# A sample's products in five matmuls instead of six: 126 rows in two planes of s, with 14 rows moved by DMA

## The reference, cut to what matters

```
a   = relu(group_norm(conv1x1(x, w1)))                       # 256 channels
om  = conv3x3(a, w_off) + b_off                               # 27 channels: 9 dx, 9 dy, 9 masks
for each tap k of 9 and pixel p:
    sampled[:, k, p] = mask[k, p] * bilinear(a, p + tap k + (dy, dx)[k, p])   # 0 outside
out = relu(group_norm(einsum(sampled, w2)))
out = relu(group_norm(conv1x1(out, w3)) + x)
```

## Time and profile before

| | us |
|---|---|
| median of 3 runs | 2962.01 (2961.58 to 2963.43) |
| the profiled execution | 2961.04 |
| its span, first to last instruction | 2958.8 |

### The profile page before, as it was taken

The page is one execution under the profiler, slowest core; times in us unless marked ns, Lnnn a source line. Parts: engine busy times, 40 slices in busy tenths (PEclk is TensorE's granted clock), DMA queues, the critical chain, the costliest instruction groups (busy, mean ns, idle before and its releaser), DMA issues.

```text
span 2958.8 us, 46593 instructions
## 1 busy us (share of the span) xinstructions
PE 2908.3 (98%) x16518; PEld 2865.9 (97%) x16518; DVE 2366.0 (80%) x5000; ACT 1795.0 (61%) x3281; POOL 455.3 (15%) x305
## 2 busy tenths in 40 slices
PE   9999999999998999999999999999999999999997
PEld 9999999999997899999999999999999999999997
DVE  5655889865666688888888888888888888888885
ACT  4544332346665466767666676676766767667664
POOL 0000000000000122221222212222122221222210
PEclk9999999999999899999999999999999999999998
DMA  7774111035663344444444444444544444444431
GB/s 270 215 238 134 44 44 40 10 124 218 245 232 130 122 136 152 156 150 158 150 153 154 148 159 151 153 155 150 158 150 156 152 149 159 148 152 156 149 121 74
DMA packets 209208, 437.39 MB, mean 148 GB/s; under 512 B 18640, under 2 KB 170192, under 8 KB 203344
## 3 DMA queue, kind: packets, MB, share of 16 engines
q1 hardware_dynamic: 159408, 326.82, 32.7%
q10 hardware_dynamic: 49568, 107.60, 11.8%
HBM read 307.71 MB, written 126.64 MB: 147 GB/s over the span
## 4 chain that ended last, share of the span: by engine, by line
PE 63%; DVE 3%; DMA 1%; ACT 1%; SPq 0%; issue 0%; POOL 0%; ACTq 0%; DVEq 0%; POOLq 0%
PE sample L87 7%; PE deform L87 7%; PE sample L88 7%; PE sample L92 7%; PE deform L92 7%; PE deform L88 6%; PE work L87 6%; PE work L92 6%; PE work L88 6%; PE work L74 1%; PE work L76 1%; PE work L75 1%; DMA hats<-hat_scratch 1%; PE work L2046 1%; DVE x L1715 1%; DVE s_lo L1819 1%
## 5 line engine op out<-in xcount | busy, mean ns | idle before, releaser
L1465 ACT ACTIVATE v_hi<-sample 128x392 fp32r<-128x392 f32 (+1 forms) x640 | 291.7, 463 | 315.1 <-PE sample L92 306.0
L87 PE MATMUL sample<-s_hi,aT_hi 98*128 98x392 f32 (+1 forms) x1280 | 417.5, 331 | 8.9 <-DVE v_lo L1827 8.9
L1675 POOL TENSOR_TENSOR hats<-hats 98x784 f32<-98x784 f32 x160 | 341.0, 2131 | 523.1 <-DMA hats<-hat_scratch 504.3
L88 PE MATMUL sample<-s_hi,aT_lo 98*128 98x392 f32 (+1 forms) x1280 | 413.3, 328 | 0.0
L87 PE MATMUL deform<-v_hi,w_w 128*128 128x392 f32 x1152 | 403.5, 350 | 0.0
L88 PE MATMUL deform<-v_hi,w_w 128*128 128x392 f32 x1152 | 393.1, 341 | 0.0
L1827 DVE TENSOR_TENSOR v_lo<-sample,v_hi 128x392 fp32r<-128x392 f32 (+1 forms) x640 | 326.9, 518 | 66.5 <-ACT v_hi L1465 62.2
L92 PE MATMUL sample<-s_lo,aT_hi 98*128 98x392 f32 (+1 forms) x1280 | 315.1, 327 | 0.0
L92 PE MATMUL deform<-v_lo,w_w 128*128 128x392 f32 x1152 | 310.4, 342 | 0.0
L1456 ACT ACTIVATE s_hi<-hats 98x784 fp32r<-98x784 f32 x288 | 245.4, 852 | 98.5 <-DVE x L1715 71.7
L1819 DVE TENSOR_TENSOR s_lo<-hats,s_hi 98x784 fp32r<-98x784 f32 x288 | 281.1, 976 | 2.4 <-ACT s_hi L1456 1.4
(11 more groups left out here) (227 smaller groups left out, 7282.9 us busy)
## 6 DMA issues: line engine op xcount, KB each, us to landing
hats<-hat_scratch SPq DMA_DIRECT2D x768, 150.1 KB
x<-in_x SPq DMA_DIRECT2D x64, 784.0 KB, 5.8
in_home<-y_scratch ACTq DMA_DIRECT2D x248, 196.0 KB, 3.3
out<-x ACTq DMA_DIRECT2D x62, 784.0 KB, 4.4
y_home<-in_x SPq DMA_DIRECT2D x32, 784.0 KB, 5.0
y_scratch<-y_out SPq DMA_DIRECT2D x16, 1568.0 KB, 5.9
terms<-in_x SPq DMA_DIRECT2D x30, 784.0 KB, 4.7
y_scratch<-y_home SPq DMA_DIRECT2D x15, 1568.0 KB, 5.1
```

The costliest lines, as they stand in the source:

```text
L87: nc.tensor.matmul(out, w_hi, x_hi, start=start, stop=False)
L88: nc.tensor.matmul(out, w_lo, x_hi, start=False, stop=False)
L1465: nc.scalar.activation(v_hi[:, group % 2, c, 0:taps_of(g), i, :], sample[:, t % 2, 0:cols(g)].rearrange("p (k s) -> p k s", s=PIX), ACT.Co ...
L1675: nc.gpsimd.tensor_tensor(hats[:, slot, 0:2, 0:n], hats[:, slot, 0:2, 0:n], hats[:, slot, 2:3, 0:n].broadcast_to([HALF, 2, n]), ALU.mult). ...
```

## The change

The 196 pixels are cut 126 + 70 (`UPPER` 9 rows of y, `LOWER` 5) instead of 98 + 98. `hats`, `s_hi` and `s_lo` keep two planes, now of 126 rows: plane 0 the upper 126 pixels, plane 1 the lower 70 and, in rows 70 to 125, the first 56 of those again. `aT` has four planes: a_hi upper, a_lo upper, [a_hi lower; a_lo lower's first 56], [a_hi lower; a_lo lower's last 14]. A tile is then five matmuls of 126, 126, 126, 126 and 84 rows, 588 in all. What stands in the same rows of another plane has to change its partition, and a DMA does that: `copy_s` moves 14 rows of s_hi (392 elements each) into s_lo's plane 1 once per unit, `copy_aT` moves a_lo's rest in two DMAs per image, out of `aT_rest`, which lies in the space of a_f. A unit's hats take four DMAs instead of three, unit 8's eight instead of six. `part_aT` and `rest_aT` are two instructions each. The fifth matmul of a unit's first tile waits for the copy of s. Two semaphores for it, and one for aT, are taken over from the first layer (`used_before`; the hunks that hand them over are left out here).

```diff
-ROWS = SIDE // 2
+UPPER = 9
+LOWER = SIDE - UPPER
+A_ROWS = UPPER * SIDE
+R_ROWS = LOWER * SIDE
+TWICE = A_ROWS - R_ROWS
+C_ROWS = R_ROWS + R_ROWS - TWICE
...
-        aT_hi = sb("aT_hi", [HALF, 2, 2, CMID], F32R)
-        aT_lo = sb("aT_lo", [HALF, 2, 2, CMID], F32R)
+        aT = sb("aT", [A_ROWS, 2, 4, CMID], F32R)
...
-        hats = sb("hats", [HALF, HATS, 3, 2 * PIX])
-        s_hi = sb("s_hi", [HALF, 2, 2, 2 * PIX], F32R)
-        s_lo = sb("s_lo", [HALF, 2, 2, 2 * PIX], F32R)
...
+        hats = sb("hats", [A_ROWS, HATS, 3, 2 * PIX])
+        s_hi = sb("s_hi", [A_ROWS, 2, 2, 2 * PIX], F32R)
+        s_lo = sb("s_lo", [A_ROWS, 2, 2, 2 * PIX], F32R)
...
+        aT_rest = a_f[0:R_ROWS, :, :, 0:P].bitcast(F32R)
...
-            return 48 * (lap + 1 + (p.n + u // (UNITS - 1) if slot == HATS - 1 else 0))
+            return 64 * (lap + 1 + (p.n + u // (UNITS - 1) if slot == HATS - 1 else 0))
...
+                parts = [(i, slice(0, n))]
...
+                    parts = [(i, slice(i * PIX, (i + 1) * PIX)) for i in range(2)]
+                for i, at in parts:
+                    n = at.stop - at.start
+                    y_hat, x_hat = (hats_at[p.n % 2, e, i, :, t0:t0 + n] for e in range(2))
+                    for dst, rows in ((hats[:, slot, 0, at], slice(0, UPPER)), (hats[0:R_ROWS, slot, 1, at], slice(UPPER, SIDE)),
+                                      (hats[R_ROWS:A_ROWS, slot, 1, at], slice(UPPER, SIDE - 1))):
+                        sp.dma_start(dst, y_hat[rows].unsqueeze(1).broadcast_to([rows.stop - rows.start, SIDE, n])
                                      ).then_inc(hats_loaded[slot], 16)
-                    return
-                for half in range(2):
-                    src = hats_at[p.n % 2, 0, i, half * ROWS:(half + 1) * ROWS, t0:t0 + n]
-                    sp.dma_start(hats[:, slot, half, 0:n], src.unsqueeze(1).broadcast_to([ROWS, SIDE, n])
+                    sp.dma_start(hats[:, slot, 2, at], x_hat.unsqueeze(0).broadcast_to([UPPER, SIDE, n])
                                  ).then_inc(hats_loaded[slot], 16)
-                src = hats_at[p.n % 2, 1, i, :, t0:t0 + n]
-                sp.dma_start(hats[:, slot, 2, 0:n], src.unsqueeze(0).broadcast_to([ROWS, SIDE, n])
-                             ).then_inc(hats_loaded[slot], 16)
+            @of_pair
+            def copy_s(p, u):
+                unit = UNITS * p.n + u
+                sp.wait_ge(s_lo_made, unit + 1)
+                sp.dma_start(s_lo[R_ROWS:C_ROWS, unit % 2, 1].bitcast(F32), s_hi[TWICE:R_ROWS, unit % 2, 1].bitcast(F32)
+                             ).then_inc(s_moved[unit % 2], 16)
+            @of_pair
+            def copy_aT(p, i):
+                sp.wait_ge(aT_lo_made, 2 * p.n + i + 1)
+                if i == 1:
+                    sp.wait_ge(aT_moved, aT_moved_before + 64 * p.n + 32)
+                for plane, rows in ((2, slice(0, TWICE)), (3, slice(TWICE, R_ROWS))):
+                    n = rows.stop - rows.start
+                    sp.dma_start(aT[R_ROWS:R_ROWS + n, i, plane].rearrange("p (k c) -> p k c", k=KM).bitcast(F32),
+                                 aT_rest[rows, :, i].bitcast(F32)
+                                 ).then_inc(aT_moved, 16)
 
...
+                copy_s(now, 1)
                 load_hats(now, 4)
+                copy_s(now, 2)
                 load_hats(now, 5)
+                copy_s(now, 3)
                 load_hats(now, 6)
+                copy_s(now, 4)
                 load_hats(now, 7)
                 load_x(coming, 0)
+                copy_s(now, 5)
                 load_hats(now, 8)
                 load_x(coming, 1)
+                copy_s(now, 6)
+                copy_s(now, 7)
                 store_hats(after, 1, 0)
...
                 load_hats(after, 0)
                 load_hats(after, 1)
+                copy_s(now, 8)
                 load_hats(after, 2)
+                copy_aT(after, 0)
+                copy_s(after, 0)
                 load_hats(after, 3)
+                copy_aT(after, 1)
...
-                nc.scalar.activation(aT_hi[:, i].rearrange("p h c -> p (h c)"), work[0:HALF, 2 * i, :],
+                nc.scalar.activation(aT[:, i, 0], work[0:A_ROWS, 2 * i, 0:CMID], ACT.Copy)
+                nc.scalar.activation(aT[0:R_ROWS, i, 2:4],
+                                     work[0:R_ROWS, 2 * i, CMID:2 * CMID].unsqueeze(1).broadcast_to([R_ROWS, 2, CMID]),
                                      ACT.Copy).then_inc(aT_hi_made, 1)
...
-                nc.vector.tensor_tensor(aT_lo[:, i].rearrange("p h c -> p (h c)"), work[0:HALF, 2 * i, :],
-                                        aT_hi[:, i].rearrange("p h c -> p (h c)").bitcast(F32),
+                nc.vector.tensor_tensor(aT[:, i, 1], work[0:A_ROWS, 2 * i, 0:CMID], aT[:, i, 0].bitcast(F32),
+                                        ALU.subtract)
+                rest = work[0:R_ROWS, 2 * i, CMID:2 * CMID].rearrange("p (k c) -> p k c", k=KM)
+                nc.vector.tensor_tensor(aT_rest[:, :, i], rest,
+                                        aT[0:R_ROWS, i, 2].rearrange("p (k c) -> p k c", k=KM).bitcast(F32),
                                         ALU.subtract).then_inc(aT_lo_made, 1)
...
-                for h in range(2):
-                    products_of_high(nc, sample[:, t % 2, 0:n], aT_hi[:, i, h, c * P:(c + 1) * P],
-                                     aT_lo[:, i, h, c * P:(c + 1) * P], s_hi[:, unit % 2, h, at:at + n], start=(h == 0))
+                to, a_part = sample[:, t % 2, 0:n], aT[:, i, :, c * P:(c + 1) * P]
+                high, low = s_hi[:, unit % 2, :, at:at + n], s_lo[:, unit % 2, :, at:at + n]
+                nc.tensor.matmul(to, a_part[:, 0], high[:, 0], start=True, stop=False)
+                nc.tensor.matmul(to, a_part[:, 1], high[:, 0], start=False, stop=False)
+                if t in (0, 2):
+                    pe.wait_ge(aT_moved, aT_moved_before + 64 * p.n + 32 * (i + 1))
+                nc.tensor.matmul(to, a_part[:, 2], high[:, 1], start=False, stop=False)
                 if c == 0:
                     pe.wait_ge(s_lo_made, unit + 1)
-                for h in range(2):
-                    last = product_of_low(nc, sample[:, t % 2, 0:n], aT_hi[:, i, h, c * P:(c + 1) * P],
-                                          s_lo[:, unit % 2, h, at:at + n], stop=(h == 1))
+                nc.tensor.matmul(to, a_part[:, 0], low[:, 0], start=False, stop=False)
+                if c == 0:
+                    pe.wait_ge(s_moved[unit % 2], s_moved_before[unit % 2] + 16 * (unit // 2 + 1))
+                last = nc.tensor.matmul(to, a_part[0:C_ROWS, 3], low[0:C_ROWS, 1], start=False, stop=True)
                 last.then_inc(sampled, 1)
```

33 lines of the change are left out of this document (15 added, 18 removed).

## The result

| | before | after |
|---|---|---|
| median of the runs, us | 2961.8 (4 runs) | 3466.3 (4 runs, 3463.0 to 3469.0) |
| ratio, 95% interval | | 1.170, 1.168 to 1.172 |
| profiled execution, us (span) | 2961.0 (2958.8) | 3465.6 (3463.4) |
| mean granted clock over the span | 0.994 | 0.930 |

The kernel is 505 us slower, 17%, where 233 us (8%) had been forecast; the sign was right, the time lies 186 us above the top of the range. One execution among all that are reported here, of experiment e8b, ran in a slower state (3838 us at a mean granted clock of 0.67) and is left out of its median.

What follows compares the result with a forecast made beforehand. The prediction took a 61.6 us ring, with TensorE not alone on the path, as the bound. Parts of 48.1, 6.05 and 15.0 made 69.1 us, 7.5 more, times 31 = 233, giving 3195 us; 8-in-10 range 3000 to 3280.

Steps and rivals of the forecast that it cites:

- three parts of a ring: The 61.6 us step: tile 5 to tile 16's end 43.45, then to unit 0's s_lo 5.55, then to tile 5 12.6.
- Unit 4's load: Behind image 1's aT DMAs on SP: costs nothing, as VectorE takes unit 4 after unit 2's s_lo; bound 1 us.
- aT, +0.5 us a step: Split copy on ScalarE (+0.35) and split subtraction on VectorE (+0.15) lengthen tile 16's end to unit 0's s_lo to 6.05.
- Four loads, +1.2 us of transfer, +0.77 of issue, in effect +1.2 at unit 3: A unit's fourth hats load shares DMA engines with the others, adding 1.2 us a unit; bounds 0 and 1.5.
- Unit 2's copy, 1.9 us: Between unit 2's s_lo and tile 4's fifth matmul: the copy lands 1.9 us on, so tile 5 starts after 15.0, not 12.6.
- Units 1, 3, 4, 5 and 7, nothing: Their copies cost nothing: more time in hand before the fifth matmul than unit 6 and less ahead in the queue.
- The issue of a copy, 0.45: On SP: issuing a copy of s takes 0.45 us, the x load's figure, and delays unit 3's load by that.
- Unit 6, stall 2.9 behind the x load: At tile 12's fifth matmul: the copy queues behind the second x load's 784 KB, landing 1619.6; stall 2.9 us.
- Unit 8, stall 3.8 behind loads 0 and 1: At tile 16's fifth matmul: the copy lands behind the next pair's unit 0 and 1 loads, at 1636.6; stall 3.8 us.
- The clock: Rival, 0.10: a 3.8 us stall could drop TensorE to half clock once a step, losing 2.7 us more; 3279 us.
- Copies don't queue: Rival, 0.20: each copy lands 1.9 us after issue, tiles 12 and 16 stall 0.5 each; step 63.4, total 3017 us.
- Faster: Rival, 0.10: hats loads come no later than now and nothing in flight delays a copy; step 61.0, total 2943 us.

Runs made afterwards that it cites:

- e8b: e1 with the two DMAs of aT's rest for image 0 issued ahead of unit 2's loads instead of behind them: 3096.5 us.
- e1: The changed kernel without the copies of 14 rows of s and without TensorE's wait for them: 3031.9 us.
- e2: The kernel before the change with the last of its six matmuls per tile left out, nothing else touched: 2915.9 us.
- e13: e1 with the third of a unit's four hats loads (56 rows) issued for the first three units only: 2960.4 us.
- e14: e1 with the third of a unit's four hats loads cut to an eighth of its columns: 3005.8 us.
- e10: e1 with the nine copies back in SP's list, into rows no product reads; TensorE waits for none, only ScalarE's part_s for the copy two units before: 3158.4 us.
- e9: e1 with the DMAs of aT's rest, and the waits for them, for the first pair only: 3044.3 us.
- e4: The changed kernel with ScalarE's two output stores issued later, behind write_y 0 and write_y 4: 3418.9 us.
- e7b: The changed kernel with unit 6's copy moved ahead of the second x load and unit 8's ahead of the next pair's unit 1 loads: 3252.1 us.
- e12: e11 with unit 2's copy also moved up, ahead of unit 4's loads: 3434.4 us.
- e15: e11 with ScalarE's second output store also moved, behind write_y 4: 3171.8 us.
- e6b: The changed kernel with the second product of tiles 4, 12 and 16 repeated (20, 16, 16 times) where TensorE would wait: 3364.6 us.
- e11: e7b with ScalarE's first output store issued later, behind write_y 0: 3164.9 us.

## Why the prediction was right about the sign and wrong about the size

The prediction added the step up from three parts of a ring. Measured in the traces by the same marks, as means of the steps between 1300 and 2800 us, they are:

| us a step | before | forecast | after | e1, no copies |
|---|---|---|---|---|
| end of s_lo of unit 0 to tile 5 | 12.9 | 15.0 | 19.0 | 15.6 |
| of it, to the end of s_lo of unit 2 | 11.0 | 12.84 | 12.9 | 12.7 |
| tile 5 to the end of tile 16 | 43.4 | 48.1 | 54.8 | 43.4 |
| the rest | 5.4 | 6.05 | 5.0 | 4.7 |
| step | 61.7 | 69.1 | 78.7 | 63.6 |

Of the 9.6 us a step that were missed, 4.0 lie between s_lo of unit 2 and tile 5, and 6.7 between tile 5 and tile 16; the rest of the ring came out 1.1 shorter than forecast. In the second part the stalls make 8.0 us where 6.7 were priced, matmuls at the lower clock 4.4 and the edges of stalls 1.2, where nothing was. From s_lo of unit 2 to tile 5 it is 6.1 us after (the flight of unit 2's copy is 5.7 of them), 1.9 before, and 2.9 in e1, which has no copies: there something else has grown. It is VectorE's wait for loads of hats, here before and after from 1300 to 2800 us (total, times, longest), which the point *Unit 4's load* below reads:

```profile
DVE hats L1812 <- DMA hats<-hat_scratch: 2.2, 5, 0.7
```
```profile
DVE hats L1856 <- DMA hats<-hat_scratch: 96.3, 45, 6.1
```

The runs split the 505 us another way: -46 (five matmuls, e2), +44 (aT's operations and 126 rows, e13 less e2), +45 and +26 (issue and bytes of the fourth load, e14 less e13, e1 less e14), +127 (copies issued, nobody waiting, e10 less e1), +308 (the fifth product waits for them). These are differences along one order of the edits; in another order the shares would differ, as 336 against 434 for the copies shows. Point by point:

- *Where TensorE would wait*: right for tiles 4, 12 and 16, and right that this turns a gain into a loss. Wrong in order: longest at tile 4, then 12, then 16. The 1.3 us at tile 0 did not come.
- *Five matmuls*: 2.1 us of the 3.3 lie in the ring's first part, 65 us. Measured 46.
- *aT, +0.5 us a step* in the last part of the ring: that part did not grow. 44 us are 1.4 a step, with the 126 rows, which I had priced at nothing, and they lie where unit 4's load is waited for (see *Unit 4's load*). *aT's two DMAs, nothing*: right as a cost (e9), though TensorE does wait for them; the place for this wait was not seen.
- *Four loads, +1.2 us of transfer, +0.77 of issue, in effect +1.2 at unit 3*: the place was right, since s_lo of unit 2 ended 12.9 us after that of unit 0, as forecast. Over the whole step 71 us are 2.3, and the larger part (45 of 71) is the issue and the fixed part, not the bytes on shared engines on which I had built.
- *Unit 2's copy, 1.9 us*: this step failed. Free of traffic a copy takes 2.1 us, so the bare price was good; but in its place it took 5.7. I wrote that a copy "moves behind what the same queue has in flight" and did not apply it here: unit 4's four loads stand between the copies of units 1 and 2 in the new list, and e4, with the store away, still has 4.4 us. And I never asked what ScalarE's queue sends at that moment. Its store of the output, 784 KB, stood in the earlier trace rows, used only as a bound for another transfer; e7b, with the loads out of the way, still has 4.2.
- *Unit 4's load, nothing*: this failed too. It was to be covered, as VectorE takes unit 4 up only behind s_lo of unit 2. Behind aT's DMAs and the copies of units 0 and 1 its first load is issued 8.1 us after the end of s_lo of unit 0, where it was 4.9 before, and VectorE then stands idle ahead of make_s of unit 4 in every step, 3.6 us on the mean (0.05 before; 1.3 in e1 and still 1.3 in e13 with its three loads). In the kernel after, the copy's flight hides this wait; without the copies it decides when tile 5 starts. That is why e1 is slower than e2, and why unit 2's copy could not simply be moved ahead of these loads (e12). Of the sign that the prediction gave, VectorE waiting over 1.5 us for unit 3, only 0.4 came; it waited for unit 4.
- *Units 1, 3, 4, 5 and 7, nothing*: failed for unit 3 (4.0 us behind the second store, 1.2 of stall) and, by little, unit 5 (0.4, its copy behind the first load of x). For unit 3 e4 and e15 confirm the store as the cause.
- *The issue of a copy, 0.45*: it is 0.82. Nine of them hold SP 3.3 us a step longer than priced, and e10 shows that the copies' place in SP's list costs 127 us though nobody waits for them. I had charged it at unit 3's load, and once ahead of the second load of x.
- *Unit 6, stall 2.9 behind the x load*: mechanism right, 3.7 measured, and e7b takes 2.0 of it away by passing that load. *Unit 8, stall 3.8 behind loads 0 and 1*: mechanism right, 2.3 measured, gone in e7b. These two make 4.3 of the 7.1 us a step that e7b gains; tile 4 gives 1.8, the clock comes back in part (171 of 1500 us at the lower level for 300), and tile 0 takes 1.9 back, waiting for aT.
- *The clock*, a rival of 0.10: it should have been a term of the sum. Its condition, a stall of 3.8 us a step, was met by my own forecast. It takes 3.3 us a step by e6b, where I had priced 2.7. The slow matmuls alone count 6.1; that a wait behind them gives part of it back is argued, not shown. I had reckoned with one fall a step, and there were 54 in 19 steps.
- *Copies don't queue* (0.20): excluded, by flights of 4 to 6.4 us. *Faster* (0.10): excluded.

What was mis-sized, then, is the copies: 14.0 us a step measured (434 / 31), where my terms at tiles 4, 12 and 16 came to about 8. In these 14 are the wait at tile 4 with unit 4's loads and the store ahead, SP's 0.82, and the clock. The bound of 1 us for a late load of unit 4 was too small as well. What each tile's stall is worth of the 308 us is open, since the phase of the step moves with each edit (e11 freed unit 2's copy, not unit 3's). No version of the changed kernel beat the kernel before: e13, without copies and with three loads, only equals it. That the change could gain with its rows moved in another way than by DMA was not tried.

## What to carry to other kernels

Price a small DMA that a matmul waits for by what every queue has in flight at its place, its own queue included, not by its own bytes: here 2.1 us became 4.0 behind 784 KB from another engine's queue, 4.4 behind four loads of its own, and 5.7 behind both. Count what its issue, and its wait in an in-order list, do to the loads behind it: moving a copy ahead of an x load gained, moving one ahead of the loads that VectorE needs next lost 269 us. When something is put ahead of a load, ask again whether the cover that the load had is still there. And where a forecast has TensorE stall for some microseconds in each step, put the fall of the clock into the sum.

## What the runs showed of the hardware

- A DMA of 14 rows of 1568 bytes from SBUF to SBUF takes 2.1 us from issue to landing when nothing is in its way and SP issues it (1.47 to its first packet, 0.44 from the start of its last packet to its landing), and 1.8 at its shortest from POOL, although no HBM is touched; SP is held 0.82 us by it, but 0.48 by a load of 784 KB.
- A store issued 0.29 us later on another queue went ahead of it, its first packet coming 0.85 us after its issue. The store's last packet ended at 1919.57, and the copy's first started at 1919.42.
- Between 1300 and 2800 us of the kernel after, the granted clock fell 54 times, each time in or just behind a stall of 1.7 to 6.2 us; with the three longest stalls of a step filled with matmuls that serve nothing (e6b) it fell 6 times.
- A fourth DMA with an eighth of the bytes still cost 45 us over 31 steps, 1.5 us a step for ten issues.
